# A decoder layer's attention: operand stacks turned by DMA instead of by TensorE

## The reference

```
q, k, v = split(x @ w_qkv.T); rope(q), rope(k); 16 heads of 16, q and k halved -> 32 sub-heads of 8
out = sdpa(q1, k1) - lam * sdpa(q2, k2)          # scores + additive mask, softmax
x = layernorm(x + group_norm(out) @ wo.T)        # self-attention, "A" below
x = layernorm(x + cross_attention(x, ctx, ctx))  # 32 query heads of 8, 8 key heads, "C" below
x = layernorm(x + moe(x))                        # 8 experts, top 2, and 2 shared ones
```

## Time and profile before

| | us |
|---|---|
| median of 3 runs | 847.19 |
| profiled execution | 847.25 |
| its span | 845.0 |
| attention stage, up to the first transposes of the experts (L1675) | 430.14 |
| full turns in it (copies L508 of 98.57 to 366.40) | 267.83 |

### The profile page before, as it was taken

One profiled execution on the slowest core, in us unless ns is written; L12 is line 12 of the kernel. 1 busy time (PEld: TensorE's weight loads), 2 busy tenths in 40 slices (PEclk: granted clock), 3 DMA queues, 4 the chain that ended last, 5 costly groups with the idle time before them and its releaser, 6 DMA issues.

```text
span 845.0 us, 19993 instructions
## 1 busy us (share of the span) xinstructions
PE 773.2 (92%) x7621; PEld 508.9 (60%) x7621; DVE 521.2 (62%) x1188; ACT 519.8 (62%) x948; POOL 308.9 (37%) x481
## 2 busy tenths in 40 slices
PE   6888999999999999997869899999999999999993
PEld 5555555555555555554435455557878888787652
DVE  3346788888888888865338866764444444444353
ACT  2445788888888888775425554545555655555353
POOL 3134455555555555544210573001222222222222
PEclk9998999999999999998569999999999999999998
DMA  8800000000010100000033676422332322223231
GB/s 247 246 2 1 2 2 33 3 24 11 2 33 2 33 2 2 2 2 1 1 97 97 194 233 201 150 89 51 47 50 45 52 45 49 48 45 52 54 104 63
DMA packets 38282, 51.02 MB, mean 60 GB/s; under 512 B 9264, under 2 KB 33072, under 8 KB 38192
## 3 DMA queue, kind: packets, MB, share of 16 engines
q1 hardware_dynamic: 31040, 40.39, 16.1%
q0 software_dynamic: 7152, 9.34, 6.6%
HBM read 31.04 MB, written 18.68 MB: 59 GB/s over the span
## 4 chain that ended last, share of the span: by engine, by line
PE 39%; DVE 5%; DMA 3%; ACT 2%; issue 1%; POOL 0%; ACTq 0%; POOLq 0%; DVEq 0%
PE ps L1684 34%; PE ps L1763 3%; DMA wst<-in_wx 3%; DVE wr L224 1%; PE ps L1743 1%; DVE ht_lo L1561 1%; DVE th L1556 1%; ACT wr L215 1%; PE ps L1675 0%; ACT th L1402 0%; DVE xg_lo L1549 0%; ACT ht_hi L1407 0%; POOL e_rs L1376 0%; PE ps L1709 0%; ACT xg_hi L1394 0%
## 5 line engine op out<-in xcount | busy, mean ns | idle before, releaser
L1363 POOL DMA_INDIRECT acc<-y_sb,xin x39 | 60.5, 1552 | 220.0 <-ACT y_sb L1431 220.0
L1684 PE MATMUL ps<-wr,xr_hi 128*128 x624 | 129.3, 299 | 0.0
L1402 ACT ACTIVATE th<-ps 128x384 f32<-128x384 f32 (+1 forms) x118 | 57.9, 491 | 108.6 <-PE ps L1684 103.6
L1684 PE MATMUL ps<-xg_hi,wsh 128*128 128x512 f16 x320 | 103.2, 385 | 4.8 <-DVE xg_lo L1549 4.8
L680 DVE TENSOR_REDUCE c_qs<-ps 128x4 f16<-128x512 f32 x128 | 84.0, 693 | 22.6 <-PE ps L937 21.0
L680 DVE TENSOR_REDUCE a_qs<-ps 128x4 f16<-128x512 f32 x128 | 85.1, 689 | 19.7 <-PE ps L937 18.7
L1684 PE MATMUL ps<-wr,xr_lo 128*128 x312 | 93.4, 299 | 0.0
L514 ACT ACTIVATE a_pt<-ps 128x512 f32<-128x512 f32 x128 | 74.5, 595 | 30.4 <-PE ps L954 28.5
L1556 DVE SCALAR_TENSOR_TENSOR th<-th,ps 128x384 f32<-128x384 f32 (+1 forms) x118 | 65.2, 553 | 34.5 <-ACT th L1402 34.4
L514 ACT ACTIVATE c_pt<-ps 128x512 f32<-128x512 f32 x128 | 69.8, 604 | 19.3 <-PE ps L954 19.1
L1643 DVE COPY ht<-ps 128x512 f16<-128x512 f16 x39 | 16.5, 424 | 93.7 <-PE ps L1763 93.7
(11 more groups left out here) (211 smaller groups left out, 1751.1 us busy)
## 6 DMA issues: line engine op xcount, KB each, us to landing
wst<-in_wx SPq DMA_DIRECT2D x30, 640.0 KB, 4.6
xs<-zero SPq DMA_DIRECT2D x1, 5031.0 KB, 19.9
xin<-xs SPq DMA_DIRECT2D x39, 129.0 KB, 2.1
acc<-x_row SPq DMA_DIRECT2D x4, 512.0 KB, 3.3
x_row<-acc SPq DMA_DIRECT2D x8, 256.0 KB, 5.2
out<-x_row SPq DMA_DIRECT2D x8, 256.0 KB, 2.1
x_row<-in_x SPq DMA_DIRECT2D x1, 1536.0 KB, 10.8
wst<-in_wqkvT SPq DMA_DIRECT2D x1, 768.0 KB, 4.8
```

The costliest lines, as they stand in the source:

```text
L1363: pool.indirect_dma_start(acc, bass.IndirectOffsetOnAxis(ap=row, axis=0), y_sb[:, n % 2, :], None, compute_op=ALU.add).then_inc(f_acc, 16)
L1402: act.activation(th[:, k % 2, 0:n], gate[:, k % 2, 0:n], ACT.Silu, scale=1.0 / WSCALE).then_inc(f_th, 1)
L1684: ins = pe.matmul(o, l[x], r[y], start=(first and n == 0), stop=(last and n == m - 1), skip_group_check=not (first and last))
```

## The change

All 96 turnings (16 batches, six each) become transposing DMAs of 128 x 1024 float16 from SBUF to SBUF, issued by SP (`turn`, `dma_start_transpose`). `stack_T`, `qm_in`, `kt_in`, `reqt_in` and their entries in `RINGS` go. `kt` gets two buffers, taken by the batch's parity, so that the key's turning waits for `exp_scores` of the batch before last. ACT's fills now wait for the DMA's completion where they waited for PE's reading. SP gets a `body(n)` of its own. The rest of its work is moved in between: the load of x's batches 4 to 15 goes behind the first two turnings, the first two weight pieces and the row numbers into turn 2, the other pieces into turns 7, 9, 11 and 13, and the zeros of `xs` are cut into 13 DMAs of 3 tiles, one in each of turns 3 to 15.

```diff
-    (1, (("aqT", 1, 0), ("akT", 1, 0), ("v", 1, 0), ("xT", 0, 0), ("qk", 0, 0), ("are", 1, 0))),
-    (1, (("rt", 7, 0), ("cre", 4, 0), ("x2T", 6, 0), ("ckT", 3, 0), ("cqT", 3, 0))),
+    (1, (("v", 1, 0), ("xT", 0, 0), ("qk", 0, 0))),
+    (1, (("rt", 7, 0), ("x2T", 6, 0))),
...
-            t.qm, t.qt, t.kt = (sb(p + n, [P, NC, P], F16) for n in ("qm", "qt", "kt"))
+            t.qm, t.qt = (sb(p + n, [P, NC, P], F16) for n in ("qm", "qt"))
+            t.kt = sb(p + "kt", [P, 2, NC, P], F16)
...
+            def turn(dst, src, done):
+
+                sp.dma_start_transpose(out=dst, in_=src[:].rearrange("p j s -> p (j s)")).then_inc(done, 16)
+
+            def stack_q(t, b):
+
+                sp.wait_ge(t.s_qlo, b + 1)
+                if b:
+                    sp.wait_ge(t.s_maxfill, FILLS * b)
+                turn(t.qm[:], t.qs, t.s_qm_in)
+
+            def stack_k(t, b):
+
+                sp.wait_ge(t.s_klo, b + 1)
+                if b >= 2:
+                    sp.wait_ge(t.s_expfill, FILLS * (b - 1))
+                turn(t.kt[:, b % 2, :, :], t.ks, t.s_kt_in)
+
+            def restack(t, b):
+
+                sp.wait_ge(t.s_maxed, FILLS * b + FILLS)
+                if b:
+                    sp.wait_ge(t.s_expfill, FILLS * b)
+                turn(t.qt[:], t.qs, t.s_reqt)
...
+            def body(n):
+
+                if live(n - 1):
+                    stack_q(A, n - 1)
+                    stack_k(A, n - 1)
+                if n == 1:
+                    sp.dma_start(x_all[:, 4:B, :], xv[:, 4:B, :]).then_inc(s_x[2], 16)
+                if live(n - 4):
+                    restack(C, n - 4)
+                if n == 2:
+                    shared_piece(0)
+                    shared_piece(1)
+                    row_numbers()
+                k, half = divmod(n - SHARED_HIGH, 2)
+                if half == 0 and 2 <= k < NSH * 3:
+                    shared_piece(k)
+                if 0 <= n - 3 < TILES // ZT:
+                    zero_rows(n - 3)
+                if live(n - 3):
+                    stack_k(C, n - 3)
+                    stack_q(C, n - 3)
+                if live(n - 1):
+                    restack(A, n - 1)
...
                 act.wait_ge(A.s_rope, b + 1)
                 if b:
-                    act.wait_ge(A.s_reT, b)
+                    act.wait_ge(A.s_reqt, 16 * b)
...
-                    pe.wait_ge(t.s_qm_in, b + 1)
-                    pe.wait_ge(t.s_kt_in, b + 1)
+                    pe.wait_ge(t.s_qm_in, 16 * b + 16)
+                    pe.wait_ge(t.s_kt_in, 16 * b + 16)
...
-                    ins = pe.matmul(score_bank(t, "m", b, f)[:, j * P:(j + 1) * P], t.qm[r, c, :], t.kt[r, c, :],
+                    ins = pe.matmul(score_bank(t, "m", b, f)[:, j * P:(j + 1) * P], t.qm[r, c, :], t.kt[r, b % 2, c, :],
```

More of the change, by code:

```diff
@@ L64 @@
 SHARED_HIGH = 3
+ZT = 3
 class Steps:
@@ new lines, in row_numbers, with zero_rows @@
+            def row_numbers():
+                sp.wait_ge(s_pset, 11)
+                sp.dma_start(zero[:, E:E + 1], a["pad_row"]).then_inc(s_rowno, 16)
+                sp.dma_start(x_row[:, :, E], a["acc_row"], allow_slow_non_contiguous=True).then_inc(s_rowno, 16)
+            def zero_rows(k):
+                if k == 0:
+                    sp.wait_ge(s_rowno, 32)
+                ts = slice(k * ZT, (k + 1) * ZT)
+                sp.dma_start(xs.rearrange("(n p) c -> p n c", p=P)[:, ts, :],
+                             zero[:].unsqueeze(1).to_broadcast([P, ZT, RW])).then_inc(s_zero, 16)
@@ L283, in _ @@
+            for n in range(ITERATIONS):
+                body(n)
+            sp.wait_ge(s_zero, 16 * TILES // ZT)
         @block.gpsimd
@@ L578, in body @@
                     cross_q_high(n - 3)
-                    kt_in(C, c_one, n - 3)
                 if live(n - 4):
@@ L898, in project_v @@
                              lambda c: wq_lo[:, c, 2 * E:], EC).then_inc(A.s_vp, 1)
-            def stack_T(src, one, s):
-                s16 = src[:].rearrange("p (c i) s -> p c (i s)", i=NI)
-                d16 = one.bitcast(F16)
-                for c in range(NC):
-                    ins = pe.transpose(d16[:, c * P:(c + 1) * P], s16[:, c, :], id16[:])
-                ins.then_inc(s, 1)
-            def stack_q(t, one, b):
-                if t is A and b == 0:
-                    pe.wait_ge(s_const, 16 * N_CONST)
-                pe.wait_ge(t.s_qlo, b + 1)
-                turns.wait(pe, "aqT" if t is A else "cqT", b)
-                stack_T(t.qs, one, t.s_qT)
-            def stack_k(t, one, b):
-                pe.wait_ge(t.s_klo, b + 1)
-                turns.wait(pe, "akT" if t is A else "ckT", b)
-                stack_T(t.ks, one, t.s_kT)
-            def restack(t, one, b):
-                pe.wait_ge(t.s_maxed, FILLS * b + FILLS)
-                turns.wait(pe, "are" if t is A else "cre", b)
-                stack_T(t.qs, one, t.s_reT)
             def max_scores(t, b, f):
                 if f == 0:
-                    pe.wait_ge(t.s_qm_in, b + 1)
-                    pe.wait_ge(t.s_kt_in, b + 1)
+                    pe.wait_ge(t.s_qm_in, 16 * b + 16)
+                    pe.wait_ge(t.s_kt_in, 16 * b + 16)
                 turns.wait(pe, "am" if t is A else "cm", b, f)
```

79 lines of the change are left out of this document (12 added, 67 removed).

## The result

The changed kernel takes 858.31 us (median of 4 runs, 856.38 to 862.61), the kernel before 847.58 on the same chip: a ratio of 1.0147, 95% interval 1.0117 to 1.0177. The profiled execution has a span of 855.8 us against 845.0 before; its mean granted clock is 0.919 against 0.961.

A forecast was written before the change was run, and what follows sets the result against it. The prediction took the turn-to-turn dependency loop, stretched by queued DMA landings, as the bound, with PE's work a floor. From 847 it added 37 (loop), 9 (C's second turning) and 7 (start and end): 900 us, range 805 to 1020.

The forecast's parts named there:

- 13.35 + Lk + Lre: Period of one attention turn: fixed parts 4.10 and 9.25 us plus two turnings; forecast 24.68 us, 2.46 more than before.
- Lk: Time from readiness of A's keys to landing of their turning DMA, SP's queue included; forecast 5.64 us against 4.47.
- Lre: Time from data readiness of A's second turning to its DMA's landing, SP's queue included; forecast 5.69 us against 4.40.
- X: Transfer time of one 256 KB transposing DMA; taken as 2.5 us, geometric mean of 1.0 and 6.4.
- T: Step by which the next DMA in SP's queue is behind: transfer plus 0.37 us of issue, 2.87 us.
- L: Landing time of a turning DMA after its issue: transfer plus 1.1 us, forecast 3.6 us.
- C's second turning: Outside the loop, but PE's list waits for it: +9 us in 13 turns; at the end +1.2, +1.6 and +1.4.
- The start: First turn, from keys ready to A's first maxima: 5.64 us in place of 2.84, so +2.8.
- Zeros and pieces moved: SP's zeros and weight pieces, placed behind C's second turning: cost nothing, or up to 1.5 us a turn if queue full.
- The clock: Rival, chance 0.13: PE 77% busy, granted clock falls to 0.74, PE's list becomes the bound; 913 to 935 us, say 920.
- 32-byte pieces: Rival, chance 0.15: turning cuts each transfer into small pieces, 6.4 us each; SP's queue is the bound, time 1150 us.
- a plain copy's speed: Rival, chance 0.30: turning DMAs transfer in 1.0 us, PE's list bounds turns at some 19.6 us, time 808 us.

## Why the prediction was right and wrong, point by point

- **The loop is what counts, 13.35 + Lk + Lre: right for a calm turn.** The two fixed parts measured 4.10 and 9.06, and with one buffer for the keys Lk grew by the wait that was worked out. PE's own list is not the bound, as was said; it is busy 18.41 us of a calm turn's 20.94, against 20.98 of 22.22 before, 2.6 less where 3.3 were counted.
- **The transfer X = 2.5, and with it the queue's step T = X + 0.37 = 2.87: the step that failed.** X is 1.4 by the row above, nearer to the lower bound of 1.0, and SP issues the next DMA 1.3 us after the first (219.31, 220.63, 222.02): the issue runs beside the transfer and is not added to it. Lk is 3.88 in place of 5.64, Lre 3.90 in place of 5.69, so the turn's +2.46 became -1.28. The landing, L = 3.6, was near, 3.1 to 3.3, because what lies around the transfer is 1.7 and not the 1.1 taken from a plain copy. By the prediction's own sign, X under 1.9, the forecast failed as a whole. Its last paragraph had this case, T short and L long, with a turn of 20.6 and a time near 825; an undisturbed turn comes near it, and it was not given a chance of its own.
- **C's second turning, +9 in the turns and +1.2 and +1.6 in the end: mis-sized both ways.** With short steps it is issued at 222.02 and lands in time in the calm turns; in the end PE waits 2.57 and 2.81 us, and the two stretches grew by 3.7 and 0.9. The 4.7 us of the end's first stretch, at half clock, stood in no term.
- **The start, +2.8: +1.4** from the first keys to the first maxima.
- **Zeros and pieces moved, at nothing: right as far as PE's waits show.** C's keys, which stand behind them, land late in 12 of 16 batches, up to 7.2 us after the issue, and in the full turns nobody waits for these.
- **The clock, a rival with 0.13, argued away because low shares came with whole turns of gaps: wrong in kind.** PE's share in the full turns did fall, from 94% to 86%, but a calm turn has 88% at a clock of 1.00; the clock fell in single spells behind single waits: 0.90 us at one place was followed by 13.8 us at the 1.2 GHz level. The prediction had landings as one number and put their spread at nothing, without a reason; those that PE waits for came in 3.0 to 5.1 us. Of the other rivals, 32-byte pieces are out by the 1.4 us of transfer; a plain copy's speed was right that X is under 1.9 and the turn shorter than 22.22, and wrong in the 19.6 us of the turn and in the time. (That 19.6 does not follow from its own terms either: 18.9 at 94% are 20.1, which would make the time 815 and not 808.)

So the time is slower for another reason than the forecast's, and the right sign was luck. Eleven turns at the calm 20.94 would be 14.2 us less than before, where the forecast had the turns longer. Late landings and the half clock behind them gave 11.2 of this back (slow turns follow landings made late by hand, and with both second turnings back on PE the eleven turns have none); the end is 9.1 longer, by waits on landings and by half clock in its first stretch. Why that stretch ran at half clock is open.

## What to carry to other kernels

A transfer that replaces work on a loop has to be judged by its late landings too and not by its median alone, since a loop without slack passes each on, and here the half clock behind it made 0.7 us into 5.4. Look at which transfers can stay: here the fastest kernel left the four first turnings to the DMA and gave the two second ones, for which PE itself stands waiting, back to PE; A's keys stayed with the DMA though they stand in the loop, and landed in 3.3 us or less in all 16 batches. Two transfers in a queue need not add up: look for the time between issues and for the landing apart. If a change gives PE less to do and the turns get shorter only in part, list the turns one by one; the mean hides that most gained and a few lost.

## What the runs showed of the hardware that was not expected

- A transposing DMA of 256 KB from SBUF to SBUF holds SP's queue for 1.23 to 1.29 us in the median and for 2.5 at most, and lands after 3.1 in the median; a plain one of the size, to DRAM, took 0.37 and 2.1.
- It is not there before its last part is: a late one spent 0.4 us at 7 GB/s near its end, with some 20 pieces open and the last of the others coming in one by one. 16 KB put on another queue beside it made two turnings 0.4 and 0.6 us late.
- After one wait of 0.90 us ahead of A's exponentials PE ran 13.8 us at a granted clock of 0.51, the 1.2 GHz level, though it was busy all through; after one of 1.98 us ahead of A's maxima the clock stayed at 1.00, and so it did behind waits of 0.67 to 1.03 us ahead of A's exponentials where PE had extra matmuls to do. Which waits bring it down was not settled.
